# Attention chunk states computed in four 32-row tiles of 36 columns, with TensorE's batch loop written out

## The reference, cut to what matters

```
x = x + 0.5 * ffn(layernorm(x));  x = x + attn(layernorm(x));  x = x + 0.5 * ffn(layernorm(x))

attn: 16 heads of E = 8;  q = elu(q * E**-0.5) + 1.0001;  k = elu(k) + 1.0001
for each token t, head h:
    kv_s[h] += outer(k_t[h], v_t[h])      # E x E
    k_s[h]  += k_t[h]                     # E
    out_t[h] = (q_t[h] @ kv_s[h]) / (q_t[h] . k_s[h] + 1e-6)
out = concat(out) @ W_out + b_out
```

## Time and profile before

| | us |
|---|---|
| median of 3 runs | 613.49 |
| lowest, highest | 611.41, 614.47 |
| the profiled execution | 610.65 |
| its span (first to last instruction) | 608.9 |
| TensorE busy | 444.8 |
| VectorE busy | 345.6 |
| GpSimd busy | 331.3 |
| ScalarE busy | 237.6 |

### The profile page before, as it was taken

One profiled execution on the slowest core, in us unless ns is written; L12 is line 12 of the kernel. 1 busy time (PEld: TensorE's weight loads), 2 busy tenths in 40 slices (PEclk: granted clock), 3 DMA queues, 4 the chain that ended last, 5 costly groups with the idle time before them and its releaser, 6 DMA issues.

```text
span 608.9 us, 12872 instructions
## 1 busy us (share of the span) xinstructions
PE 444.8 (73%) x4788; PEld 297.6 (49%) x4788; DVE 345.6 (57%) x984; ACT 237.6 (39%) x629; POOL 331.3 (54%) x259
## 2 busy tenths in 40 slices
PE   1884966997699325899999979149867599857970
PEld 1742543553345213677777768148335355433440
DVE  6396971221115992687777865485999222212097
ACT  4971212332224277555555530187611133322420
POOL 6184776888786601222222220004987788887691
PEclk9987875555569657799999986656978555555995
DMA  8998600101009980001111110541000000100592
GB/s 267 375 250 323 232 9 9 9 5 10 7 5 377 408 317 0 2 3 39 36 34 35 34 36 10 156 177 57 2 0 9 8 8 6 10 6 6 174 409 107
DMA packets 34389, 60.40 MB, mean 99 GB/s; under 512 B 12611, under 2 KB 18846, under 8 KB 33870
## 3 DMA queue, kind: packets, MB, share of 16 engines
q1 hardware_dynamic: 23078, 58.41, 26.8%
q0 software_dynamic: 11264, 1.38, 2.6%
HBM read 37.43 MB, written 29.36 MB: 110 GB/s over the span
## 4 chain that ended last, share of the span: by engine, by line
DVE 29%; PE 29%; issue 15%; DMA 13%; ACT 7%; POOL 5%; SPq 1%; POOLq 0%; DVEq 0%; another core or an unknown queue 0%; ACTq 0%
DVE X L973 9%; DMA rows_d<-A 5%; PE bank L897 5%; PE bank L778 4%; PE bank L878 4%; PE bank L795 3%; POOL planes_d L438 3%; DVE Cb L1075 3%; ACT A L508 3%; DMA planes_d<-Bb,put_i 2%; POOL A L452 2%; DVE bn L978 2%; DMA Bb<-planes_d 2%; PE bank L768 2%; PE bank L788 2%
## 5 line engine op out<-in xcount | busy, mean ns | idle before, releaser
L438 POOL DMA_INDIRECT planes_d<-Bb,put_i x64 | 100.4, 1569 | 24.6 <-issue 18.4
L452 POOL DMA_INDIRECT A<-rows_d,tok_i x64 | 71.9, 1124 | 20.6 <-issue 16.6
L1105 DVE TENSOR_TENSOR ring<-ring,bank 128x88 f32<-128x88 f32 x64 | 15.7, 246 | 103.7 <-ACT ring L576 72.0
L675 PE MATMUL bank<-ident,A 128*128 128x128 f32 x96 | 22.5, 412 | 55.1 <-ACT A L508 40.9
L479 POOL TENSOR_TENSOR Bb<-Cb,chm 128x576 f32<-128x576 f32 x16 | 19.0, 1220 | 66.8 <-DVE Cb L1139 33.4
L768 PE MATMUL bank<-ident,A 128*128 128x128 f32 x64 | 30.0, 469 | 29.3 <-DMA A<-rows_d,tok_i 23.2
L396 POOL TENSOR_TENSOR Bb<-Eb,st 128x512 f32<-128x512 f32 x8 | 8.9, 1112 | 74.7 <-DVE st L1023 74.7
L570 ACT ACTIVATE ring<-bank 128x128 f32<-128x128 f32 x64 | 17.7, 277 | 81.4 <-PE bank L768 70.7
L675 PEld LDWEIGHTS bank<-ident,A 128*128 128x128 f32 x96 | 18.2, 220 | 58.1 <-issue 29.9
L479 POOL TENSOR_TENSOR Bb<-w3s,chm 128x576 f32<-128x576 f32 x16 | 17.8, 1147 | 49.8 <-PE bank L920 49.8
L795 PE MATMUL bank<-w2s,ring 88*64 88x128 f32 x256 | 43.9, 446 | 0.0
(11 more groups left out here) (155 smaller groups left out, 1121.6 us busy)
## 6 DMA issues: line engine op xcount, KB each, us to landing
planes_d<-zeros SPq DMA_DIRECT2D x8, 2048.0 KB, 20.6
w3s<-in_w3T SPq DMA_DIRECT2D x2, 2816.0 KB
rows_d<-A SPq DMA_DIRECT2D x8, 512.0 KB, 11.5
A<-planes_d SPq DMA_DIRECT2D x8, 512.0 KB, 9.2
PL<-planes_d SPq DMA_DIRECT2D x8, 512.0 KB, 10.1
Cb<-planes_d SPq DMA_DIRECT2D x8, 512.0 KB, 10.8
Bb<-planes_d SPq DMA_DIRECT2D x8, 512.0 KB, 12.0
w1s<-in_w1T SPq DMA_DIRECT2D x1, 2816.0 KB
```

The costliest lines, as they stand in the source:

```text
L438: pool.indirect_dma_start(out=planes_d[f], in_=Y[:, s, :], in_offset=None, out_offset=bass.IndirectOffsetOnAxis(ap=put_i[:, s:s + 1], axis=0),
L452: pool.indirect_dma_start(out=A[:, t, :], out_offset=None, in_=rows_d, in_offset=bass.IndirectOffsetOnAxis(ap=tok_i[:, t:t + 1], axis=0), ...
L675: ins = pe.transpose(bank[g % 2][:, (i % 4) * P:(i % 4 + 1) * P], A[:, i, :], ident[:, :])
```

## The change

The chunk states are made in column tiles. For each chunk, four matmuls with 32 weight columns (the keys of four heads, partitions 32j to 32j+31 of the result) and 36 moving columns (the values and ones of the same four heads) take the place of one with 128 and 144. A part's four chunks then fit into one bank, 36 columns each. VectorE masks within the four heads by `hm` and adds, on 144 columns per part where it was 576. The use of the states follows: four groups g, each 32 rows of queries and of states, 36 moving columns. Groups 0 and 2 go first, to banks 4 and 5, then TensorE waits for them on a new semaphore, then groups 1 and 3 go to the same banks. A step has 60 matmuls for the states where it had 15, and 60 for their use where it had 30. TensorE's loop over the batches is written out, with waits against constants; the other engines keep their loops.

```diff
+    GW = 4 * (E + 1)
-    AFTER = ((), (0, 1, 2), (3, 4), (5, 6, 7))
+    AFTER = ((), (0, 1), (2,), (3,))
...
-                    for m in AFTER[g]:
-                        q = m // 2
-                        if m >= len(STATES):
-                            pe.wait_ge(kv_sb, PRIMED + NH * b + m + 1 - len(STATES))
-                        for k in range(1 if m == NH - 1 else 2):
-                            ins = pe.matmul(bank[STATES[m % len(STATES)]][:, k * VW:(k + 1) * VW], KN[:, 2 * (m % 2) + k, q, :],
-                                            VN[par][:, q, :, :].rearrange("p h f -> p (h f)"), start=True, stop=True)
+                    for q in AFTER[g]:
+                        if q >= len(STATES):
+                            pe.wait_ge(kv_sb, PRIMED + NQ * b + q + 1 - len(STATES))
+                        for c in range(NC if q < NQ - 1 else NC - 1):
+                            for j in range(4):
+                                ins = pe.matmul(bank[STATES[q % len(STATES)]][32 * j:32 * j + 32, c * GW:(c + 1) * GW],
+                                                KN[:, c, q, 32 * j:32 * j + 32],
+                                                VN[par][:, q, 4 * j:4 * j + 4, :].rearrange("p h f -> p (h f)"),
+                                                start=True, stop=True)
                         ins.then_inc(kv_ps, 1)
...
-                for half in range(2):
+                for g in (0, 2, 1, 3):
+                    rows = slice(32 * g, 32 * g + 32)
+                    if g == 1:
+                        pe.wait_ge(even_ps, b + 1)
                     for c in range(NC):
                         for q in range(NQ):
...
-                            ins = pe.matmul(bank[4 + half][32 * q:32 * q + 32, c * HV:(c + 1) * HV], QT[par][:, t0:t0 + CHUNK],
-                                            before_c[:, half * HV:(half + 1) * HV], start=False, stop=True, skip_group_check=True)
+                            ins = pe.matmul(bank[4 + g // 2][32 * q:32 * q + 32, o:o + GW], QT[par][rows, t0:t0 + CHUNK],
+                                            before_c, start=False, stop=True, skip_group_check=True)
+                    if g == 2:
+                        ins.then_inc(even_ps, 1)
...
-            with pe.Fori(0, (B - 2) // 2) as i:
-                step(2 * i + 1, 1)
-                step(2 * i + 2, 0)
-            step(B - 1, 1, last=True)
+            for b in range(1, B):
+                step(b, b % 2, last=b == B - 1)
...
-                        dve.tensor_tensor(SW[:, q, 2 * (m % 2):2 * (m % 2) + n, :],
-                                          bank[STATES[m % len(STATES)]][:, 0:n * VW].rearrange("p (c v) -> p c v", c=n),
-                                          own[:, :].unsqueeze(1).broadcast_to([P, n, VW]), ALU.mult).then_inc(kv_sb, 1)
+                        dve.tensor_tensor(SW[:, q, 0:n, :].rearrange("p c (j f) -> p c j f", j=4),
+                                          bank[STATES[q % len(STATES)]][:, 0:n * GW].rearrange("p (c j f) -> p c j f", c=n, j=4),
+                                          hm[:, :].unsqueeze(1).unsqueeze(3).broadcast_to([P, n, 4, E + 1]),
+                                          ALU.mult).then_inc(kv_sb, 1)
```

More of the change, by code:

```diff
@@ L67, in macaron_kernel @@
     QS = float(E) ** -0.5
-    NH = 2 * NQ
     STATES = (0, 2, 1)
-    AFTER = ((), (0, 1, 2), (3, 4), (5, 6, 7))
+    AFTER = ((), (0, 1), (2,), (3,))
     ctx = ExitStack()
@@ L165, in macaron_kernel @@
         HTB, KT, QT0 = (Bb[:, o + k * L:o + (k + 1) * L] for k in range(3))
-        SW = Cb[:, 0:NQ * NC * VW].rearrange("p (q c v) -> p q c v", q=NQ, c=NC)
+        SW = Cb[:, 0:NQ * NC * GW].rearrange("p (q c v) -> p q c v", q=NQ, c=NC)
         VN0 = Cb[:, o:o + NQ * VW]
@@ L253, in macaron_kernel @@
         o_ps = sem("o_ps")
+        even_ps = sem("even_ps")
         o_step = sem("o_step")
@@ L626, in copy_kn @@
                 act.wait_ge(kn_ps, b + 1)
-                act.wait_ge(kv_ps, PRIMED + NH * b)
+                act.wait_ge(kv_ps, PRIMED + NQ * b)
                 for c in range(NC):
@@ L828, in project @@
                 if not (isinstance(b, int) and b == 0):
-                    pe.wait_ge(kv_sb, PRIMED + NH * (b - 1))
+                    pe.wait_ge(kv_sb, PRIMED + NQ * (b - 1))
                     pe.wait_ge(q_read, 2 * b)
@@ L910, in step @@
                                   VX[:, q, h, :, :], start=(h % 8 == 0), stop=False, skip_group_check=True)
-                pe.wait_ge(kv_sb, PRIMED + NH * (b + 1))
+                pe.wait_ge(kv_sb, PRIMED + NQ * (b + 1))
                 pe.wait_ge(sb_ready, (NQ - 1) * (b + 1))
-                for half in range(2):
+                for g in (0, 2, 1, 3):
+                    rows = slice(32 * g, 32 * g + 32)
+                    if g == 1:
+                        pe.wait_ge(even_ps, b + 1)
                     for c in range(NC):
@@ L918, in step @@
                             t0 = q * P + c * CHUNK
-                            before_c = SW[:, q, c - 1, :] if c else SW[:, q - 1, NC - 1, :]
-                            ins = pe.matmul(bank[4 + half][32 * q:32 * q + 32, c * HV:(c + 1) * HV], QT[par][:, t0:t0 + CHUNK],
-                                            before_c[:, half * HV:(half + 1) * HV], start=False, stop=True, skip_group_check=True)
+                            before_c = SW[rows, q, c - 1, :] if c else SW[rows, q - 1, NC - 1, :]
+                            o = c * HV + (g % 2) * GW
+                            ins = pe.matmul(bank[4 + g // 2][32 * q:32 * q + 32, o:o + GW], QT[par][rows, t0:t0 + CHUNK],
+                                            before_c, start=False, stop=True, skip_group_check=True)
+                    if g == 2:
+                        ins.then_inc(even_ps, 1)
                 ins.then_inc(o_ps, 1)
@@ L1137, in value @@
                     dve.wait_ge(vx_ready, PRIMED + NC * (b - 1))
-                    dve.wait_ge(kv_ps, PRIMED + NH * (b - 1))
+                    dve.wait_ge(kv_ps, PRIMED + NQ * (b - 1))
                 dve.tensor_tensor(VN[par][:, :, :, 0:E],
@@ L1170, in step @@
                                       ALU.mult).then_inc(sc_sb, 1)
[L1171 to L1174, removed]
-                        dve.tensor_tensor(SW[:, q, 2 * (m % 2):2 * (m % 2) + n, :],
-                                          bank[STATES[m % len(STATES)]][:, 0:n * VW].rearrange("p (c v) -> p c v", c=n),
-                                          own[:, :].unsqueeze(1).broadcast_to([P, n, VW]), ALU.mult).then_inc(kv_sb, 1)
-                        if q and m % 2:
-                            n = NC if q < NQ - 1 else NC - 1
-                            dve.wait_ge(kv_sb, PRIMED + NH * b + 2 * q + 2)
+                    for q in AFTER[g]:
+                        n = NC if q < NQ - 1 else NC - 1
+                        dve.wait_ge(kv_ps, PRIMED + NQ * b + q + 1)
+                        dve.tensor_tensor(SW[:, q, 0:n, :].rearrange("p c (j f) -> p c j f", j=4),
+                                          bank[STATES[q % len(STATES)]][:, 0:n * GW].rearrange("p (c j f) -> p c j f", c=n, j=4),
+                                          hm[:, :].unsqueeze(1).unsqueeze(3).broadcast_to([P, n, 4, E + 1]),
+                                          ALU.mult).then_inc(kv_sb, 1)
+                        if q:
+                            dve.wait_ge(kv_sb, PRIMED + NQ * b + q + 1)
                             if q > 1:
@@ L1184, in step @@
                             dve.tensor_tensor(SW[:, q, 0:n, :], SW[:, q, 0:n, :],
-                                              SW[:, q - 1, NC - 1:NC, :].broadcast_to([P, n, VW]), ALU.add).then_inc(sb_ready, 1)
+                                              SW[:, q - 1, NC - 1:NC, :].broadcast_to([P, n, GW]), ALU.add).then_inc(sb_ready, 1)
                 if not last:
```

## The result

| | before | changed |
|---|---|---|
| median, us | 612.45 (4 runs, 610.78 to 614.47) | 624.58 (4 runs, 623.91 to 626.52) |
| the profiled execution, us | 610.65 | 626.52 |
| its span, us | 608.9 | 624.8 |

The change makes the kernel slower: ratio 1.0202, 95% interval 1.0159 to 1.0244. Forecast were 592 us and a range of 585 to 606.

A forecast was written before the change was run, and what follows sets the result against it. TensorE bounds the attention steps, VectorE close behind. Batches 1 to 6 give -17.5 us, batch 0 -2.45, batch 7 -1.0, together -21: 589.7 for the profiled execution, 592 against the median; range 585 to 606.

The forecast's parts named there:

- The loop written out: TensorE's batch loop as straight code: costed at nothing, with bounds of -0.3 and +0.3 us per step.
- States on TensorE: Making the chunk states per step: 60 small matmuls at L909's 9.8 ns per record, 1.33 us for 4.13, -2.80.
- Use of the states: L920, queries times states, per step: 60 matmuls of 32 rows, 1.65 us against 1.20, +0.45.
- Rival 1: New 32-row L920 tiles don't pack or gain partly lost: 600 us, 24%; both new kinds slow: 621 us, 5%.
- VectorE and the wait for L1155: VectorE's masks and adds shrink 3.5 us per step; TensorE's 0.58 us idle before the key transposes goes.
- Batch 7: Last batch, at the low clock: states save 5.45 us, later groups fall into the low stretch; net -1.0.
- Rival 2: TensorE's clock falls in every step as small tiles replace large matmuls between the scores: about 620 us, 7%.

The follow-up runs named there:

- experiment 2: The kernel before with only TensorE's batch loop written out; 609.72 us, ratio 0.9999.
- short loop: The changed kernel with a TensorE loop of one step, ScalarE copying queries and values to a fixed place, batch 7 behind the loop; 606.5 us, ratio 0.9898 to before.
- experiment 4: The kernel before, loop and tiles kept, with 30 unused one-column matmuls added per step behind L909; 640.2 us, ratio 1.0465.
- experiment 6: The kernel before with TensorE's loop written out and 75 unused one-column matmuls added per step; 655.79 us, ratio 1.0692.
- experiment 8: The short loop with batch 7 inside the loop too, every engine preparing an unused next batch; 597.99 us, ratio 0.9805 to the kernel before.
- the loop of 532 matmuls: The changed kernel with TensorE's loop of two steps back and an added semaphore step around the use of the states; 643.36 us, ratio 1.0547 to the kernel before.
- experiment 5: The kernel before, its loop kept, with 15 unused one-column matmuls added per step; 613.85 us, ratio 1.0062.

## Why the prediction was wrong, point by point

**The step that failed** is "The loop written out", with its sentence "I cost it at nothing; the instruction stream is longer, and batch 0, also fetched for the first time, shows no stall." For the loop written out *by itself* that is right, experiment 2. But the sentence took batch 0 of before as evidence for the changed step. Batch 0 of before has 183 matmuls (it lacks `turn_out` and `project_out`) and 14.9 us from its states to those of batch 1. The change raises a step from 191 to 266 matmuls and shortens it from 15.7 to 12.8 us at once, from one 16 KB block per 5.4 us to one per 3.1, and most of them stand in its dense half. What the runs showed in place of the zero is 18.5 us per step where 12.87 is possible. The profile of before had no row at that rate, and I gave this resource no bound but 0.3 us per step: the page showed the queue, and I didn't ask how many bytes a matmul takes. The term needed was the supply of instructions for the matmuls that stand close together.

**The size of it.** Six steps of the changed kernel, batch 1 to batch 7, take 110.8 us; six of 12.87, as in the short loop, would take 77.2. Of the 33.6 us between them, 13.6 are pieces of issue of 0.3 us or more, which leaves 20, nearly all for the same matmuls at 1.2 GHz. The granted clock agrees: from 273.93 to 384.73 it is 0.79, so (1 - 0.79) / 0.5 = 42% of the time is at the low level, of 110.8 us 47, and at most half of that is lost, 23. So the lower clock is the larger part of the loss. It follows the gaps: with the same matmuls and no gap the clock is 1.00 (experiment 7), and with gaps it falls even where the large states are kept (0.92 from 252 to 358 in experiment 4, 0.85 in 6). Against the 94.4 us of six steps of 15.74 us the changed kernel comes out 16.4 longer, which is the whole 15.9 us of the spans.

**States on TensorE**, forecast 1.33 us for 4.13: 0.70 + 0.40 + 0.33 = 1.43 in the changed kernel where no gap falls, slightly more in the short loop (0.76). Right.

**Use of the states**, forecast 1.65 us, by the L909 rate and not by L878's: 0.68 + 0.14 + 0.72 = 1.54 in the short loop. Right; the 32-row tiles pack, and the wait on the first half costs 0.14 where I had 0.20. That the step came within 0.1 us of 12.8 is in part luck: the states were sized 0.1 too small and their use 0.1 too large. Rival 1 as written didn't occur.

**VectorE and the wait for L1155**: no such wait is left in the short loop's step. The gain that the prediction saw, 2.9 us per step, is there in the run where the program is there: 15.74 - 12.87 = 2.87.

**Batch 7** was forecast at the low clock with a net of -1.0. In the changed kernel it ran so (L898 x64 in 1.12 us, which is 0.70 at the high level). I had this as hardly to be changed; experiment 8 shows 6 us in it by the two ratios (0.9805 for 0.9898), 8.5 by the medians, part of it the gap of 1.90 us.

**Rival 2** had the right time (about 620) and the right sign of trouble, a granted clock of 0.5 within the steps, but the wrong mechanism, the shape of the tiles. Its "against", that no fall comes without idle time before it, held. What I overlooked is that the idle time could come from something other than a wait in the program.

What stays open: where exactly between 412 and 442 matmuls the body stops being kept; how the loss of the loop of 532 matmuls divides into gaps and clock; how many matmuls may stand close together in straight code (188 records of L909 and L920 in 2.5 us pass in experiment 2 without a gap, 218 with those of L912 don't in experiment 5); and which gaps bring the clock down. That a program supplied faster would give the straight code 12.87 us as well wasn't tried, since nothing in the kernel sets this pace.

## What to carry to other kernels

When a change trades a few large matmuls for many small ones, count the instructions too, first the matmuls of each dense stretch and then those of the whole step. Here straight code could bring 64 fp32 matmuls in 3.5 to 4.0 us and little ahead of that, so a step that has time enough in the mean can still wait in its dense half (experiment 6). A loop ran free of it from its second pass on, as long as its body stayed at 412 or less. "Issue" in the midst of a group of equal matmuls, a record count of about 128 between two such gaps, and a q8 row that grows are the marks of it; what helped is a shorter loop body, even at the price of copies that another engine makes beside it, and the last batch taken into the loop.

## What the runs showed of the hardware that I had not expected

- Between a loop's body that is kept and one that is fetched in every pass there are at most 30 matmuls: bodies of 382 and 412 gave 2 and 3 transfers of 16 KB in 62 us, all in the first pass, and 442 gave 14 and a gap of 4.4 us at each of the two returns to the loop's start, 28 us in all for 30 matmuls a step.
- In a dense stretch of straight code the gaps at TensorE's issue come 64 matmuls and 3.5 to 4.0 us apart, and a transfer that comes in time costs nothing (11 of them in experiment 2, clock 1.00).
- A gap of 0.66 us, 11 us behind one of 2.24, was followed by 1.2 GHz within a microsecond (L898 x24 0.52 us at 297.81, where the high level gives 0.33). Not every gap does this: behind one of 0.72 us at 280.82, L927 still ran at the high level. Over the six steps the low clock cost about 20 us beside 13.6 us of gaps.
- Stretches of 32x32 and 128x32 tiles hold 2.4 GHz through whole steps (window 292 to 350 of the short loop, 1.00). In the kernel before, 32x32 scores and full 128x128 states in turn didn't bring it back from 361 to 377, with TensorE busy throughout; small tiles without large ones weren't tried there.
